# Weights laid out by the host, rounded inside the linear attention, and the first softmax batch's norm moved ahead of the last spectral adds

## What is computed

```
x = x + 0.5 * tanh(ln(x) @ W1 @ W2 @ W3 + bias)     # FFN1
x = x + linear_attention(ln(x)) @ Wo + bo           # LIN, 16 heads of 8
x = x + 0.5 * tanh(ln(x) @ W1 @ W2 @ W3 + bias)     # FFN2
x = x + 0.5 * spectral(ln(x))                       # SPEC1, a product with a circulant-like matrix
x = x + softmax_attention(ln(x))                    # 16 heads of 64, causal, weights Q, K, V, W
x = x + 0.5 * spectral(ln(x))
```

## Time and profile before

| | us |
|---|---|
| median of three runs | 1265.1 (1263.7 to 1266.8) |
| the profiled execution | 1264.6 |
| its span in the trace | 1262.9 |
| TensorE busy | 1193.1 (94%) |
| VectorE busy | 1025.6 (81%) |
| ScalarE busy | 1003.5 (79%) |
| GpSimd busy | 586.6 (46%) |
| mean granted TensorE clock | 0.992 of full speed |

### The profile page before, as it was taken

How to read it: one execution, slowest core, us unless ns; L and a number is a source line. 1 busy time by engine, 2 the same in 40 slices (tenths; PEclk the granted TensorE clock), 3 DMA queues, 4 the chain that set the end, 5 groups by cost and what they waited for, 6 DMA issues and landing times.

```text
span 1262.9 us, 38370 instructions
## 1 busy us (share of the span) xinstructions
PE 1193.1 (94%) x10883; PEld 1040.7 (82%) x10883; DVE 1025.6 (81%) x4877; ACT 1003.5 (79%) x3491; POOL 586.6 (46%) x913
## 2 busy tenths in 40 slices
PE   4699977799999999999999999999999999999996
PEld 3588976678888888888888888888888888888885
DVE  6878879977788888888888888888888888888874
ACT  4866648678888888888888888888888888888884
POOL 4821137725444444444444444444444444444442
PEclk9999989999999999999999999999999999999999
DMA  8000000000000000000000000000000000000000
GB/s 222 1 1 0 1 2 1 1 2 2 3 2 9 0 8 7 1 8 0 8 0 8 0 8 0 8 0 8 0 8 0 8 0 8 0 8 0 9 2 18
DMA packets 14444, 11.81 MB, mean 9 GB/s; under 512 B 852, under 2 KB 12664, under 8 KB 14200
## 3 DMA queue, kind: packets, MB, share of 16 engines
q1 hardware_dynamic: 14240, 11.19, 3.3%
q10 hardware_dynamic: 152, 0.00, 0.0%
HBM read 7.00 MB, written 4.19 MB: 9 GB/s over the span
## 4 chain that ended last, share of the span: by engine, by line
PE 85%; DVE 4%; issue 3%; ACT 2%; POOL 2%; DMA 1%; SPq 1%; POOLq 0%; DVEq 0%; ACTq 0%
PE ps L1158 14%; PE ps L1141 13%; PE ps L1167 10%; PE ps L1127 7%; PE ps L1110 7%; PE ps L1123 6%; PE ps L1111 5%; PE ps L1112 5%; PE ps L1149 2%; PE ps L1148 2%; PE ps L1147 2%; PE ps L988 2%; PE ps L1010 1%; POOL rstd L318 1%; PE ps L1183 1%
## 5 line engine op out<-in xcount | busy, mean ns | idle before, releaser
L816 ACT ACTIVATE pr<-ps,neg_max 128x128 f32<-128x128 f32 (+1 forms) x1024 | 424.8, 430 | 110.7 <-DVE neg_max L538 110.7
L333 POOL TENSOR_TENSOR pr<-pr,rinv 128x256 f32<-128x256 f32 x256 | 157.3, 615 | 517.0 <-DVE rinv L546 517.0
L538 DVE CUSTOM_DVE_ANT_0 ps<-ps,mask 128x128 f32<-128x128 f32 (+1 forms) x1024 | 329.4, 389 | 0.5
L335 POOL TENSOR_TENSOR pr<-pr,rinv 128x512 f32<-128x512 f32 x256 | 266.2, 1040 | 0.0
L553 DVE COPY pT<-ps 128x512 f32<-128x512 f32 x256 | 176.1, 688 | 60.1 <-PE ps L1141 58.6
L816 ACT ACTIVATION_READ_ACCUMULATOR pr<-ps,neg_max 128x1 f32 x1024 | 218.0, 213 | 0.0
L1141 PE MATMUL ps<-ident,pr 128*128 128x128 f32 x1536 | 210.2, 273 | 2.5 <-POOL pr L335 1.1
L1141 PEld LDWEIGHTS ps<-ident,pr 128*128 128x128 f32 x1536 | 179.4, 141 | 21.2 <-POOL pr L335 2.6
L1158 PE MATMUL ps<-pT,space 128*64 128x256 f32 (+1 forms) x2048 | 194.9, 332 | 0.7 <-ACT pT L825 0.5
L1158 PEld LDWEIGHTS ps<-pT,space 128*64 128x64 f32 x2048 | 126.8, 136 | 55.5 <-ACT pT L825 0.7
L1110 PE MATMUL ps<-x_hi,wqk_hi 128*128 128x256 f32 x512 | 168.0, 328 | 2.4 <-issue 1.9
(11 more groups left out here) (188 smaller groups left out, 2637.0 us busy)
## 6 DMA issues: line engine op xcount, KB each, us to landing
out<-x_all SPq DMA_DIRECT2D x16, 256.0 KB, 2.3
x_all<-L_attn_x SPq DMA_DIRECT2D x1, 768.0 KB, 7.0
x_all<-L_attn_x SPq DMA_DIRECT2D x1, 512.0 KB, 5.0
...
```

The costliest lines, as they stand in the source:

```text
L333: nc.gpsimd.tensor_tensor(pr[:, buf, :, 0, :], pr[:, buf, :, 0, :], r[:, :, 0:1].to_broadcast([P, 2, P]), ALU.mult)
L335: nc.gpsimd.tensor_tensor(pr[:, buf, :, 1:3, :].rearrange("p h b k -> p h (b k)"), pr[:, buf, :, 1:3, :].rearrange("p h b k -> p h (b k)") ...
L538: last = nc.vector.tensor_tensor_reduce(o, o, mask[:, T - w:T], -1.0, -MASKED, ALU.add, ALU.min, neg_max[:, j, 2 * h + qt:2 * h + qt + 1])
L816: last = nc.scalar.activation(dst, ps[:, BANK_S + 2 * j + h, qt * P:qt * P + w], ACT.Exp, bias=neg_max[:, j, at:at + 1], scale=-1.0, accum ...
```

## The change

The host hands the weights over in the layout that the products need. `laid_out` transposes W1, W2 and Wd, lays out Q, K, V as [channel, head x 64] and W as pairs of heads. The transposes, their evictions and GpSimd's rearranging copy go; Q, K, V and W are loaded as 128 rows of 1024 floats instead of 64 of 2048 (W as 128 of 1024 before too).

The high and low parts of Q, K, V and the scaled W are now made from SBUF, in turns of the linear attention. `early` is keyed by (stage, turn), and is looked up ahead of the turns behind the loop too. ScalarE: two 512-column copies each ahead of LIN turns 0, 1 and 10 (high parts of Q, K, V), and two behind LIN turn 11, ahead of turn 12 (`wz`). VectorE: one 1024-column operation each ahead of LIN turns 1 and 10, and one behind LIN turn 11, ahead of turn 12.

The norm of the first two batches moves into the last turns of SPEC1 on VectorE: statistics of batch 0 ahead of turn 13, its normalisation and the statistics of batch 1 ahead of turn 14, the normalisation of batch 1 ahead of turn 15. The first batch's transposes go to bank 7 and stand directly behind the last spectral product. Statistics of batches 0 and 1 wait for the first add of SPEC1 alone; `values` of batch 0 wait for the adds whose banks they take.

```diff
-    for stages in plan:
+    for k, stages in enumerate(plan):
         for t in range(-LEAD, 2):
             if t < 0:
                 turn(before, G + t)
-            if t in early and not before:
-                early[t]()
+            if (k, t) in early:
+                early[k, t]()
             turn(stages, t)
...
         for t in range(2 * last, G - LEAD):
+            if (k, t) in early:
+                early[k, t]()
             turn(stages, t)
         before = stages
     for t in range(G - LEAD, G):
+        if (k, t) in early:
+            early[k, t]()
         turn(before, t)
...
-        q_raw, k_raw, v_raw = (space[0:DQ, k * D * H:(k + 1) * D * H] for k in range(3))
-        w_raw = space[:, 3 * D * H:3 * D * H + DV * H]
-        w_heads = space[:, 3 * D * H + DV * H:3 * D * H + 2 * DV * H]
-
-        wt_s = sb("wt_s", [P, 3, D])
+        qk_weights, v_weights, out_weights = space[:, 0:2 * H * DQ], space[:, 2 * H * DQ:3 * H * DQ], space[:, 3 * H * DQ:4 * H * DQ]
...
-        FIRST_V_BANKS = (BANK_X, BANK_T)
+        FIRST_X_BANK, FIRST_V_BANKS = BANK_Y, (BANK_X, BANK_T)
...
-                    for dst, src in ((bd_s[:], bd.unsqueeze(1)), (wd_s[:], Wd), (wu_s[:], Wu), (wq_s[:], Wq), (wo_s[:], Wo),
+                    for dst, src in ((bd_s[:], bd.unsqueeze(1)), (wdT_s[:], Wd), (wu_s[:], Wu), (wq_s[:], Wq), (wo_s[:], Wo),
...
-            sp.dma_start(q_raw, Q.rearrange("q d h -> q (d h)")).then_inc(in_qk, 16)
-            sp.dma_start(k_raw, K.rearrange("q d h -> q (d h)")).then_inc(in_qk, 16)
-            sp.dma_start(v_raw, V.rearrange("q d h -> q (d h)")).then_inc(in_vw, 16)
-            sp.dma_start(w_raw, W.rearrange("d v h -> d (v h)")).then_inc(in_vw, 16)
+            sp.dma_start(qk_weights[:, 0:H * DQ], Q).then_inc(in_qk, 16)
+            sp.dma_start(qk_weights[:, H * DQ:], K).then_inc(in_qk, 16)
+            sp.dma_start(v_weights, V).then_inc(in_v, 16)
+            sp.dma_start(out_weights, W).then_inc(in_w, 16)
...
-            pool.wait_ge(in_vw, 32)
-            nc.gpsimd.tensor_copy(w_heads.rearrange("d (h v) -> d h v", h=H),
-                                  w_raw.rearrange("d (v h) -> d h v", h=H)).then_inc(w_heads_ready, 1)
...
-                stats(b + SOFT, lambda t: xb(b, t, 1), BT, j, 4 * G)
+                stats(b + SOFT, lambda t: xb(b, t, 1), BT, j, 4 * G if above_0(b - 1) else 3 * G + 1)
...
-            def qk_weights_low():
-
-                for i in range(4):
-                    dve.wait_ge(su_hi, count(i + 1))
-                    at = slice(512 * (i % 2), 512 * (i % 2) + 512)
-                    nc.vector.scalar_tensor_tensor(out=wqk_lo[:, i // 2, at], in0=ps[:, i, :], scalar=QK_SCALES[i // 2],
-                                                   in1=wqk_hi[:, i // 2, at].bitcast(F32),
-                                                   op0=ALU.mult, op1=ALU.subtract).then_inc(su_lo, 1)
-
-            def v_low():
-
-                for i in range(2):
-                    dve.wait_ge(su_hi, count(4 + i + 1))
-                    nc.vector.tensor_tensor(v_lo[:, 512 * i:512 * i + 512], ps[:, V_BANKS[i], :],
-                                            v_hi[:, 512 * i:512 * i + 512].bitcast(F32), ALU.subtract).then_inc(su_lo, 1)
-
-            ln_soft_stats(0, 0)
-            ln_soft_norm(0, 0)
-            ln_soft_stats(1, 1)
-            qk_weights_low()
-            x_low(0, 0)
-            v_low()
-            ln_soft_norm(1, 1)
+            def qk_weights_low(s):
+
+                dve.wait_ge(su_hi, 2 * s + 2)
+                at = slice(s * H * DQ, (s + 1) * H * DQ)
+                nc.vector.scalar_tensor_tensor(out=wqk_lo[:, s, :], in0=qk_weights[:, at], scalar=QK_SCALES[s],
+                                               in1=wqk_hi[:, s, :].bitcast(F32), op0=ALU.mult, op1=ALU.subtract).then_inc(su_lo, 1)
+
+            def v_weights_low():
+
+                dve.wait_ge(su_hi, 6)
+                nc.vector.tensor_tensor(v_lo[:], v_weights, v_hi[:].bitcast(F32), ALU.subtract).then_inc(su_lo, 1)
+
+            def first_norm():
+                ln_soft_norm(0, 0)
+                ln_soft_stats(1, 1)
+
+            phases(dve, [[(3, g_norm(FFN1)), (5, g_stats(FFN1)), (0, add_tanh(0))],
+                         [(1, context_mask), (1, phi_q), (4, g_norm(LIN)), (5, g_stats(LIN)), (3, x_lin_low), (2, phi_k), (1, z_and_y),
+                          (0, add_bank(mm_done, G, lambda j: LIN_O))],
+                         [(3, g_norm(FFN2)), (5, g_stats(FFN2)), (0, add_tanh(1))],
+                         [(3, g_norm(SPEC1)), (5, g_stats(SPEC1)), (0, add_bank(mm_done, 3 * G, lambda j: BANK_OUT + j))]],
+                   early={(0, -2): bias_parts, (0, 1): bias_of_keys_values,
+                          (1, 1): lambda: qk_weights_low(0), (1, G - LEAD - 1): lambda: qk_weights_low(1), (2, -LEAD): v_weights_low,
+                          (3, G - 3): lambda: ln_soft_stats(0, 0), (3, G - 2): first_norm, (3, G - 1): lambda: ln_soft_norm(1, 1)})
+
+            x_low(0, 0, FIRST_X_BANK)
...
+            nc.scalar.copy(w23[:], ps[:, 2, 0:D]).then_inc(su_ev, 1)
...
-            def qk_weights_high():
-
-                for i in range(4):
-                    act.wait_ge(su_pe, count(6 + i))
-                    nc.scalar.mul(wqk_hi[:, i // 2, 512 * (i % 2):512 * (i % 2) + 512], ps[:, i, :], QK_SCALES[i // 2]).then_inc(su_hi, 1)
-
-            def v_high():
-
+            def qk_weights_high(s):
+
+                act.wait_ge(in_qk, 32)
                 for i in range(2):
-                    act.wait_ge(su_pe, count(10 + i))
-                    nc.scalar.copy(v_hi[:, 512 * i:512 * i + 512], ps[:, V_BANKS[i], :]).then_inc(su_hi, 1)
+                    at = slice(512 * i, 512 * i + 512)
+                    nc.scalar.mul(wqk_hi[:, s, at], qk_weights[:, 1024 * s + 512 * i:1024 * s + 512 * i + 512], QK_SCALES[s]).then_inc(su_hi, 1)
+
+            def v_weights_high():
+
+                act.wait_ge(in_v, 16)
+                for i in range(2):
+                    at = slice(512 * i, 512 * i + 512)
+                    nc.scalar.copy(v_hi[:, at], v_weights[:, at]).then_inc(su_hi, 1)
 
             def w_out():
+                act.wait_ge(in_w, 16)
                 for i in range(2):
-                    act.wait_ge(su_pe, count(12 + i))
-                    nc.scalar.mul(wz[:, 4 * i:4 * i + 4, :].rearrange("p h d -> p (h d)"), ps[:, W_BANKS[i], :], OUT_SCALE).then_inc(su_ev, 1)
+                    nc.scalar.mul(wz[:, 4 * i:4 * i + 4, :].rearrange("p h d -> p (h d)"), out_weights[:, 512 * i:512 * i + 512],
+                                  OUT_SCALE).then_inc(su_ev, 1)
...
-                   early={0: small_out})
-
-
-            def x_high(b, j):
+                   early={(0, 0): small_out, (1, 0): lambda: qk_weights_high(0), (1, 1): lambda: qk_weights_high(1),
+                          (1, G - LEAD - 1): v_weights_high, (2, -LEAD): w_out})
...
-            qk_weights_high()
-            x_high(0, 0)
-            v_high()
-            w_out()
+            x_high(0, 0, FIRST_X_BANK)
...
-            tr(ps[:, 0, 0:D], w123_s[:, 0, :], ident[:])
-            tr(ps[:, 0, D:2 * D], w123_s[:, 1, :], ident[:]).then_inc(su_pe, 1)
+            mm(ps[:, 2, 0:D], w123_s[:, 1, :], w123_s[:, 2, :], start=True, stop=True).then_inc(su_pe, 1)
             pe.wait_ge(su_ev, 1)
-            mm(ps[:, 2, 0:D], wt_s[:, 1, :], w123_s[:, 2, :], start=True, stop=True).then_inc(su_pe, 1)
+            mm(ps[:, 3, 0:D], w123_s[:, 0, :], w23[:], start=True, stop=True).then_inc(su_pe, 1)
             pe.wait_ge(su_ev, 2)
-            mm(ps[:, 3, 0:D], wt_s[:, 0, :], w23[:], start=True, stop=True).then_inc(su_pe, 1)
...
-                tr(ps[0:R, 2, 0:D], wd_s[:], ident[:])
-
...
-            def qk_weights():
-
-                pe.wait_ge(in_qk, 32)
-                for i in range(4):
-                    raw = (q_raw, k_raw)[i // 2].rearrange("q (d h) -> q h d", h=H)
-                    for h in range(H // 2):
-                        last = tr(ps[:, i, h * DQ:(h + 1) * DQ], raw[:, (i % 2) * (H // 2) + h, :], ident[0:DQ, 0:DQ])
-                    last.then_inc(su_pe, 1)
-
-            def v_weights():
-
-                pe.wait_ge(in_vw, 32)
-                v_h = v_raw.rearrange("v (d h) -> v h d", h=H)
-                for h in range(H):
-                    last = tr(ps[:, V_BANKS[h // 8], (h % 8) * DV:(h % 8 + 1) * DV], v_h[:, h, :], ident[0:DV, 0:DV])
-                    if h % 8 == 7:
-                        last.then_inc(su_pe, 1)
-
-            def out_weights():
-
-                pe.wait_ge(w_heads_ready, 1)
-                pe.wait_ge(su_lo, 1)
-                for p in range(PAIRS):
-                    last = tr(ps[:, W_BANKS[p // 4], (p % 4) * D:(p % 4 + 1) * D], w_heads[:, p * P:(p + 1) * P], ident[:])
-                    if p % 4 == 3:
-                        last.then_inc(su_pe, 1)
...
-            qk_weights()
+            x_transpose(0, 0, FIRST_X_BANK)
```

(30 more changed lines are left out.)

45 lines of the change are left out of this document (17 added, 28 removed).

## The result

The changed kernel takes 1256.57 us (median of 4 runs, 1256.06 to 1257.7) against 1264.65 of the kernel before on the same chip. The ratio is 0.9933, 95% interval 0.9922 to 0.9945; a second set of runs gave 0.9936 (0.9919 to 0.9953). The span of the profiled execution fell from 1262.9 to 1254.8.

What follows compares the result with a forecast made beforehand. TensorE, busy 94% of the span, was taken to bound the kernel, other engines mattering where it waits. Profiled 1264.6 - 6.9 (changeover) + 1.1 (roundings) = 1258.8, plus 0.5 to the median: 1259.3 us, range 1256.5 to 1262.6.

Steps and rivals of the forecast that it cites:

- The start of the program: Program start: removed transposes and copies lie ahead of VectorE's wait for x, so 0 us, +-0.5.
- The changeover: Last spectral product to first softmax query and key product: earlier norms, no weight transposes, gain 6.9 us.
- Rival 1: New changeover: the clock drops, 0.4 us lost and 1.6 added, 1261.3 us; chance 0.13.
- Rival 2: Changeover: batch 0's norms stay behind the adds, only weight work goes, gain 2.9 there, 1262.9 us; chance 0.09.
- The port lock: Spectral group 15: GpSimd's copy slows VectorE's normalisation through a shared port, 2.23 us; otherwise gain about 5.3, not 6.9.
- The roundings: Linear attention: inserted ScalarE and VectorE work costs 0.5, 0.4, 0.2 us at turns 1, 10, 12; 1.1 us in all.
- The loop's entry: Start of the loop over batches: no term in the sum; only rival 4 covers its 1.92 us gap.
- rival 4: Batch loop's start: code loading, the 1.92 us gap goes or another appears, up to 2 us each way; chance 0.06.
- The sum: Whole kernel: 1264.6 - 6.9 + 1.1 = 1258.8 us profiled, forecast 1259.3 us as median.
- The range: Whole kernel: 1256.5 to 1262.6 us, taking in a hidden insertion, a vanished gap and the low clock.
- hidden insertion: Linear attention: the inserted roundings cost TensorE nothing, -1.1 us against the forecast.
- vanished gap: Start of the loop over batches: the gap of 1.92 us goes, -1.9 us against the forecast.

Runs made afterwards that it cites:

- e_start_only: Kernel before with only the start of the program changed (two weights and Wd laid out by the host): 1265.62 us, ratio 1.0001.
- experiment 7: Changed kernel with each of VectorE's three roundings in the linear attention executed twice, first result unread: 1259.67 us, ratio 0.9953.
- experiment 8: Changed kernel with all roundings moved to the linear attention's last turn but one, timed twice: 1255.61 and 1257.14 us, ratios 0.9913 and 0.9935.
- c_before: Kernel before, unedited, profiled a second time: 1264.85 us.
- e_pad2: Changed kernel with 236 already fulfilled waits (118 instructions) added at the start of TensorE's program: 1261.88 us, ratio 0.9974.

## Why the prediction was right or wrong

- **The start of the program: 0 us.** Right: 1.0001 for it alone. The 0.8 us by which x landed earlier in the first profile after is chance; the same kernel has 7.26 and 6.25.
- **The changeover: 6.9 us.** Right, and so step by step: 6.82. Against the start of the last spectral product the forecast put the statistics of batch 0 at -3.4, its normalisation at -1.5, the last add at +1.3 and the product at +2.4 us; they came at -3.56, -1.62, +1.26 and +2.42. Rival 1, a low clock there, did not come in any of the ten profiles. The row it leans on, low clock behind 2.35 us of idle time, was one execution's: the same idle time had the full clock behind it in nine of twelve profiles. Rival 2's sum, a gain of 2.9 from the weight work alone, was 2.7. The port lock was right. What I undervalued is how low the old changeover's clock could stay: in the profile of e_start_only it lost 1.5 us more than in the first of before (0.32 in the step, 1.20 behind it).
- **The roundings: 1.1 us.** The mechanism was right, the size too big: 0.62, as 0.30, 0.15 and 0.18 for turns 1, 10 and 12 where I had 0.5, 0.4 and 0.2. The operation itself was well priced (1.22 us for 1.25). What was mis-sized is how much of a delay lands on TensorE. ScalarE's pair put yT0 off by 0.60 us in turn 1, as forecast (0.61), and by as much in turns 10 and 12, where the room on ScalarE lies behind yT0; but 0.36 to 0.43 us of it were back by the next turn's yT0. What stayed is VectorE's: experiment 7 found no cover left there. Moved to the end of the stage (experiment 8) they cost 0.1.
- **The loop's entry: 0, with 6% for a change.** This step failed: the sum has no term for it, and rival 4 gives the gap as much chance to grow as to go, without a reason for either. The gap of 1.92 us was in the profile, I had named it, and the change took 118 of TensorE's instructions out ahead of it. Mean loop step of the three profiles with an undisturbed gap (before, c_before, e_pad2): -0.33; of the ten without it: 0.83. So 1.2 us were gained here, not the whole gap, since TensorE now waits for VectorE (0.84 us in the first profile).
- **The sum.** 6.8 - 0.6 + 1.2 = 7.4 us, instead of 5.8. The second set of runs has 1264.45 - 1257.08 = 7.4, the first 8.1; the rest, up to 0.7 us, lies inside the intervals, and the low stretches (0.9 to 1.5 us each; the changeover before has one that the new one does not have) are enough to carry it. I can't settle how much of it is the old changeover's clock.
- **The range** ended at 1256.5, 0.07 us below the result, which is luck more than room. It names a hidden insertion and a vanished gap, which together reach down to 1256.3, and nothing on top of them, such as the clock of the old changeover. In the same paragraph the chances of a faster kernel add up to 0.87, not 0.86.
